# A gated cross-attention block: squared queries in bf16 halves, and the turns and the queue in a new order

## What is computed

```python
q = (layernorm(x) @ Wq).reshape(B, 100, 16, 128); k, v = ctx @ Wk, ctx @ Wv   # k, v likewise by head
q = q * rsqrt(mean(q * q, -1) + EPS) * gq
k = k * rsqrt(mean(k * k, -1) + EPS) * gk
x = x + tanh(g_xattn[0]) * (softmax(q @ k.T / sqrt(128)) @ v @ Wo)
x = x + tanh(g_ffn[0]) * bitlinear_ffn(layernorm(x))    # ternary weights, 8-bit activations
```

## Time and profile before

| | us |
|---|---|
| median of the runs | 2326.5 (2323.11 to 2329.4) |
| the profiled execution | 2321.96 |
| its span, first to last instruction | 2320.2 |
| PE busy in it | 2209.8 (95%) |
| DVE / ACT / POOL busy | 1820.5 / 1612.1 / 1265.4 |

### The profile page before, as it was taken

How to read it: one execution, slowest core, us unless ns; L and a number is a source line. 1 busy time by engine, 2 the same in 40 slices (tenths; PEclk the granted TensorE clock), 3 DMA queues, 4 the chain that set the end, 5 groups by cost and what they waited for, 6 DMA issues and landing times. The chain is left out here.

```text
span 2320.2 us, 45840 instructions
## 1 busy us (share of the span) xinstructions
PE 2209.8 (95%) x16338; PEld 1564.2 (67%) x16338; DVE 1820.5 (78%) x4171; ACT 1612.1 (69%) x3398; POOL 1265.4 (55%) x1623
## 2 busy tenths in 40 slices
PE   5799999999999999999999999999999999769999
PEld 3567777777777777777777777776777777524444
DVE  5888877777877777877787787777877777579996
ACT  4677777777776777777777677776777677446665
POOL 4555656565656565656667676766676655200000
PEclk9999999999999999999999999999999999989999
DMA  6777676766767677657776767677767665635655
GB/s 147 172 152 141 127 143 127 141 135 129 141 129 143 130 140 128 136 105 149 136 146 135 154 132 154 132 146 136 137 145 139 132 108 115 177 87 142 140 139 125
DMA packets 921748, 317.53 MB, mean 137 GB/s; under 512 B 864912, under 2 KB 882608, under 8 KB 921264
## 3 DMA queue, kind: packets, MB, share of 16 engines
q1 hardware_dynamic: 921520, 314.61, 67.5%
HBM read 82.09 MB, written 19.40 MB: 44 GB/s over the span
## 5 line engine op out<-in xcount | busy, mean ns | idle before, releaser
L893 DVE TENSOR_TENSOR khat<-keys_ps,krs 128x512 f32<-128x512 f32 (+1 forms) x384 | 263.6, 686 | 286.2 <-POOL krs L1175 286.2
L1181 POOL TENSOR_TENSOR ksplit<-khat,ksplit 128x512 bf16<-128x512 f32 (+1 forms) x384 | 444.6, 1159 | 70.7 <-ACT ksplit L667 68.7
L1175 POOL TENSOR_TENSOR krs<-kvar,minus_half 128x4 f32<-128x4 f32 (+1 forms) x384 | 387.1, 1008 | 32.0
L689 ACT ACTIVATE prob<-score_ps,nbias,qrs 100x361 f32<-100x361 f32 x512 | 329.1, 647 | 65.3 <-DVE nbias L911 63.6
L1172 POOL TENSOR_SCALAR kvar<-kss 128x4 f32<-128x4 f32 (+1 forms) x384 | 88.6, 231 | 513.6 <-DVE kss L883 511.4
L672 ACT ACTIVATE ksq<-keys_ps 128x512 f32<-128x512 f32 (+1 forms) x384 | 228.3, 596 | 196.2 <-PE keys_ps L25 196.2
L923 DVE SCALAR_TENSOR_TENSOR psplit<-prob,rden,psplit 100x361 bf16<-100x361 f32 x512 | 349.3, 690 | 5.5 <-ACT psplit L698 1.4
L698 ACT ACTIVATE psplit<-prob,rden 100x361 bf16<-100x361 f32 x512 | 304.1, 594 | 49.6 <-DVE rden L917 48.7
L23 PE MATMUL keys_ps<-wk_split,ctxT 128*128 128x512 bf16 (+1 forms) x768 | 294.5, 383 | 26.2 <-DMA ctxT<-nat 14.7
L901 DVE TENSOR_REDUCE nmax<-score_ps 100x1 f32<-100x361 f32 x512 | 268.2, 524 | 54.6 <-PE score_ps L25 54.1
L667 ACT ACTIVATE ksplit<-khat 128x512 bf16<-128x512 f32 (+1 forms) x384 | 240.5, 626 | 85.0 <-DVE khat L893 83.7
(11 more groups left out here) (132 smaller groups left out, 5256.7 us busy)
## 6 DMA issues: line engine op xcount, KB each, us to landing
stage<-in_ffn SPq DMA_DIRECT2D x96, 256.0 KB, 3.2
ctx_raw<-in_ctx SPq DMA_DIRECT2D x31, 256.0 KB, 3.4
xin<-in_x SPq DMA_DIRECT2D x32, 200.0 KB
res_rows<-in_x SPq DMA_DIRECT2D x32, 200.0 KB
x_rows<-res_rows SPq DMA_DIRECT2D x32, 200.0 KB
xin<-x_rows SPq DMA_DIRECT2D x25, 256.0 KB, 2.8
xres<-x_rows SPq DMA_DIRECT2D x25, 256.0 KB, 3.0
out<-xres SPq DMA_DIRECT2D x25, 256.0 KB, 2.0
```

The source lines that it names most:

```text
L689: act.activation(prob[:, h, :], score_ps[h % 2][0:SQ, 0:SK], ACT.Exp, bias=nbias[:, b, h:h + 1], scale=qrs[:, v // 2 % 2, r:r + 1], accum_ ...
L893: dve.tensor_tensor(khat[0:KV[t], k, :].rearrange("p (h d) -> p h d", h=G), keys_ps[k][0:KV[t], :].rearrange("p (h d) -> p h d", h=G), rs, ...
L1175: pool.tensor_tensor(krs[0:KV[t], k, :], kvar[0:KV[t], k, :], minus_half[0:KV[t], 0:G], ALU.pow).then_inc(krs_done, 1)
L1181: pool.tensor_tensor(ksplit[0:KV[t], t, 1, :], khat[0:KV[t], (u + t) % 2, :], ksplit[0:KV[t], t, 0, :], ALU.subtract).then_inc(k_lo_done, 1)
```

## The change

- **Squares in halves.** ACT squares each query half twice, once into fp32 (`qsq`, now for one half at a time) and once into bf16 (`queries_square_hi`). POOL subtracts the second from the first (`query_squares_lo`). `query_squares` then runs two bf16 matmuls a head and sample instead of one fp32 one, each with 128 columns of weights instead of 100, so that it reads 28 columns further than its data. The fp32 copy of y that is turned at a pair's end (`yT`) lies in the same memory.
- **Waits added.** `queries_lo` also waits for both squares. `queries_square` waits for POOL's low half of the half before. `scores` waits until the last `queries_lo` of its head group has freed its bank.
- **Order.** On PE, `queries(1)` stands before the third key tile and `keys(v + 2, 0)` right after it; the two mixes stand together; `query_squares` moves from in front of `heads_out` to in front of `project`; in the second turn two projections stand before the first scores. ACT, DVE and POOL follow. ACT's new order in two_turns: keys_square 0, 1; queries_hi 0, queries_square_hi 0; weight_chunk(u); queries_square 0; exp 0; keys_hi 0; queries_hi 1, queries_square_hi 1; keys_square 2; queries_square 1; keys_square(v) 0; probs_hi 0, exp 1; keys_hi 1; mixed_hi 0; keys_hi 2; mixed_hi 1; exp 2, probs_hi 1; keys_square(v) 1; exp 3; [turn_x_hi 0]; heads_out_hi 0, 1; [turn_x_hi 1]; probs_hi 2, 3; keys_square(v) 2, keys_hi(v) 0, 1; exp(v) 0, 1; keys_hi(v) 2; weight_chunk(v); probs_hi(v) 0, exp(v) 2, 3; mixed_hi(v) 0, 1; probs_hi(v) 1, 2, 3.
- **Queue.** Chunks have two buffers each way, a chunk is loaded a turn earlier and stored a turn later; context is loaded at the ends of turns 2 and 6 and turned in turns 4 and 5 behind the keys. The new buffers lie in the staging slots, of which there are now 6 instead of 7.

The core of the diff (indentation cut by 8):

```diff
 k = (AT_LAST if last else AT_LOOP)[key] + len(AT_FIRST)
 return i * USES + k, k % 2
+    def query_use(i, u):
+n = i * UNITS + u // 2 * 2 - 3
+return use(n // UNITS, ("q", n % UNITS, QD - 1))[0]
     def unit(i, u):
...
 qT_hi, qT_lo = sb("qT_hi", [P, 2, G, QT], BF16), sb("qT_lo", [P, 2, G, QT], BF16)
-qsq = sb("qsq", [P, G, QT], F32)
+qsq, qsq_split = sb("qsq", [P, TWO, QT], F32), sb("qsq_split", [P, 2 * G * QT + PAD], BF16)
+qsq_hi, qsq_lo = (qsq_split[:, a * G * QT:(a + 1) * G * QT].rearrange("p (h q) -> p h q", h=G)
+                  for a in range(2))
 psplit = sb("psplit", [SQR, QD, 2, TWO, SKF], BF16)
 oT_hi, oT_lo = sb("oT_hi", [P, G, QT], BF16), sb("oT_lo", [P, G, QT], BF16)
 assert NT == G
-yT = qsq
+yT = qsq_split[:, 0:2 * G * QT].bitcast(F32).rearrange("p (m q) -> p m q", m=NT)
 res_rows = sb("res_rows", [P, 2, DM], F32)
...
 assert CHUNK == PIECE
-w_raw, w_out = stage[:, 0, :], sb("w_out", [P, CHUNK], BF16)
-w_abs, w_part = sb("w_abs", [P, MATRICES, CHUNKS], F32), sb("w_part", [P, MATRICES], F32)
+w_raw, w_out = [stage[:, 0, :], stage[:, 3, :]], [
+    stage[:, 2, k * CHUNK // 2:(k + 1) * CHUNK // 2].bitcast(BF16) for k in range(2)]
...
+        i, u = (i, u + 1) if u < UNITS else (i + 1, 1)
         n, m = sum_chunk_of(i, u), tern_chunk_of(i, u)
-        if n is not None and n > 0:
-            sp.wait_ge(w_summed, n)
-        if m is not None:
-            sp.wait_ge(w_summed, MATRICES * CHUNKS)
-            if m > 0:
-                sp.wait_ge(w_rounded, m)
-        if n is not None or m is not None:
+        if (n if at_start else m) is not None:
+            c = n if m is None else MATRICES * CHUNKS + m
+            if m is not None:
+                sp.wait_ge(w_summed, min(c - 1, MATRICES * CHUNKS))
+                if m > 1:
+                    sp.wait_ge(w_rounded, m - 1)
+            elif n > 1:
+                sp.wait_ge(w_summed, n - 1)
             rows, cols = chunk_at(n if m is None else m)
-            sp.dma_start(w_raw[:, :], w_ffn[rows, cols]).then_inc(w_raw_in, 16)
+            sp.dma_start(w_raw[c % 2], w_ffn[rows, cols]).then_inc(w_raw_in[c % 2], 16)
...
+        m = tern_chunk_of(*((i, u - 1) if u > 1 else (i - 1, UNITS)))
         if m is not None:
             rows, cols = chunk_at(m)
             sp.wait_ge(w_rounded, m + 1)
-            sp.dma_start(w_tern[rows, cols], w_out[:, :]).then_inc(w_tern_out, 16)
+            sp.dma_start(w_tern[rows, cols], w_out[m % 2]).then_inc(w_tern_out[m % 2], 16)
     def load_ternary(u):
...
+        load_chunk(i, u, True)
         if not last and u == 1:
-            sp.wait_ge(nat_ready, (i * 2 + 2) * KVT)
-            load_ctx(i + 1, 0, ctx_raw)
             for b in range(2):
                 sp.wait_ge(xT_hi_done, i * 2 + b + 1)
                 load_x(i + 1, b, xin, x_in)
-        if not last and u == 3:
-            sp.wait_ge(nat_ready, (i * 2 + 3) * KVT)
-            load_ctx(i + 1, 1, ctx_raw)
-        if not last and u in (UNITS - 3, UNITS - 2):
-            sp.wait_ge(keys_done, tile(i, u + 1, KVT - 1) + 1)
-            turn_ctx(i + 1, u - (UNITS - 3), 1 - par)
         if has_keys(u, last):
             turn_keys(i, u + 2, 0), turn_keys(i, u + 2, 1), turn_keys(i, u + 2, 2)
+        if not last and u in (UNITS - 4, UNITS - 3):
+            sp.wait_ge(keys_done, tile(i, u + 2, KVT - 1) + 1)
+            turn_ctx(i + 1, u - (UNITS - 4), 1 - par)
         load_pieces(i, u, 0)
         if has_scores(u, last):
...
         if has_scores(u, last):
             turn_probs(i, u + 1, 1)
         load_pieces(i, u, 2)
+        if not last and u == 2:
+            sp.wait_ge(nat_ready, (i * 2 + 3) * KVT)
+            load_ctx(i + 1, 1, ctx_raw)
+        if i < PAIRS - 2 and u == UNITS - 2:
+            sp.wait_ge(nat_ready, (i * 2 + 4) * KVT)
+            load_ctx(i + 2, 0, ctx_raw)
         store_chunk(i, u)
+        load_chunk(i, u, False)
         if last:
             load_ternary(u)
...
             eng.wait_ge(kT_in[b], keys_turned(i, u))
+            eng.wait_ge(shared_free, query_use(i, u) + 1)
...
         ps = shared_bank(i, ("qss", u))
-        eng.wait_ge(q_sq_done, i * (NG * QD) + ((u + 3) // 2 + 1) * QD)
+        eng.wait_ge(q_sqlo_done, i * (NG * QD) + ((u + 3) // 2 + 1) * QD)
         for b in range(2):
             for h in range(G):
-                last = pe.matmul(ps[0:SQ, b * G + h:b * G + h + 1], qsq[:, h, b * SQ:(b + 1) * SQ],
-                                 ones[:, 0:1], start=True, stop=True)
+                out, hi, lo = ps[:, b * G + h:b * G + h + 1], h * QT + b * SQ, (G + h) * QT + b * SQ
+                pe.matmul(out, qsq_split[:, hi:hi + P], ones[:, 0:1], start=True, stop=False)
+                last = pe.matmul(out, qsq_split[:, lo:lo + P], ones[:, 0:1], start=False, stop=True)
         last.then_inc(shared_done, 1)
     def heads_out(i, u, k):
...
@@ -600,39 +627,36 @@
             queries(i, u, 0)
         if su:
             scores(i, u + 1, 0), scores(i, u + 1, 1)
+        if qu:
+            queries(i, u, 1)
         if ku:
             keys(i, u + 2, 2)
-        if qu:
-            queries(i, u, 1)
+        if kv:
+            keys(i, v + 2, 0)
         if su:
             scores(i, u + 1, 2)
-        mixed(i, u, 0, par)
+        mixed(i, u, 0, par), mixed(i, u, 1, par)
         if su:
             scores(i, u + 1, 3)
-        if kv:
-            keys(i, v + 2, 0)
-        mixed(i, u, 1, par)
         if kv:
             keys(i, v + 2, 1)
         if new_x:
             turn_x(i, 0)
-        if qu:
-            query_squares(i, u)
-        if i == TERN_PAIR - 1 and u == 1:
-            weight_totals(i)
         heads_out(i, v, 0), heads_out(i, v, 1)
         if new_x:
             turn_x(i, 1)
         if kv:
             keys(i, v + 2, 2)
+        if qu:
+            query_squares(i, u)
+        if i == TERN_PAIR - 1 and u == 1:
+            weight_totals(i)
+        project(i, v, 0), project(i, v, 1)
         if sv:
             scores(i, v + 1, 0), scores(i, v + 1, 1)
-        project(i, v, 0), project(i, v, 1)
-        if sv:
-            scores(i, v + 1, 2)
         project(i, v, 2), project(i, v, 3)
         if sv:
-            scores(i, v + 1, 3)
+            scores(i, v + 1, 2), scores(i, v + 1, 3)
         if mv:
             mixed(i, v, 0, par), mixed(i, v, 1, par)
         if v == UNITS:
...
         eng.wait_ge(shared_done, n + 1)
-        act.activation(qsq[:, k * TWO:(k + 1) * TWO, :],
-                       shared_ps[p][:, 0:TWO * QT].rearrange("p (h q) -> p h q", h=TWO),
-                       ACT.Square).then_inc(q_sq_done, 1)
+        if started(i * (NG * QD) + (u + 3) // 2 * QD + k):
+            eng.wait_ge(q_sqlo_done, i * (NG * QD) + (u + 3) // 2 * QD + k)
+        act.activation(qsq[:, :, :], ps, ACT.Square).then_inc(q_sq_done, 1)
+    def queries_square_hi(i, u, k):
+        n, p = use(i, ("q", u, k))
+        ps, heads = shared_ps[p][:, 0:TWO * QT].rearrange("p (h q) -> p h q", h=TWO), slice(k * TWO, (k + 1) * TWO)
+        eng.wait_ge(shared_done, n + 1)
+        act.activation(qsq_hi[:, heads, :], ps, ACT.Square).then_inc(q_sqhi_done, 1)
     def queries_hi(i, u, k):
...
         eng.wait_ge(q_hi_done, i * (NG * QD) + ((u + 3) // 2 * QD + k + 1))
+        eng.wait_ge(q_sq_done, i * (NG * QD) + ((u + 3) // 2 * QD + k + 1))
+        eng.wait_ge(q_sqhi_done, i * (NG * QD) + ((u + 3) // 2 * QD + k + 1))
...
@@ -1026,83 +1050,84 @@
         kv, sv, mv = has_keys(v, last), has_scores(v, last), has_mixed(v, last)
         new_x = u == UNITS - 5 and not last
         if ku:
-            sum_keys(i, u + 2, 0), scale_keys(i, u + 2, 0), sum_keys(i, u + 2, 1)
+            sum_keys(i, u + 2, 0), sum_keys(i, u + 2, 1)
         if su:
-            row_max(i, u + 1, 0), row_bias(i, u + 1, 0), row_max(i, u + 1, 1), row_bias(i, u + 1, 1)
+            row_max(i, u + 1, 0), row_bias(i, u + 1, 0), row_max(i, u + 1, 1)
+        if ku:
+            scale_keys(i, u + 2, 0)
         if qu:
             queries_lo(i, u, 0)
+        if ku:
+            scale_keys(i, u + 2, 1)
+        if su:
+            row_bias(i, u + 1, 1)
         if i == TERN_PAIR - 1 and u == 1:
             weight_sums()
-        if ku:
-            scale_keys(i, u + 2, 1), sum_keys(i, u + 2, 2)
         if su:
             row_sum(i, u + 1, 0)
         if ku:
-            scale_keys(i, u + 2, 2)
+            sum_keys(i, u + 2, 2)
+        if qu:
+            queries_lo(i, u, 1)
+        if kv:
+            sum_keys(i, v + 2, 0)
         weights_lo(pieces_of(i, u, 0))
         if su:
             row_max(i, u + 1, 2)
         if new_x:
             layernorm(i, 0)
-        if qu:
-            queries_lo(i, u, 1)
+        if ku:
+            scale_keys(i, u + 2, 2)
         if su:
-            row_max(i, u + 1, 3), row_bias(i, u + 1, 2), row_sum(i, u + 1, 1), probs_lo(i, u + 1, 0)
-            row_bias(i, u + 1, 3)
-        mixed_lo(i, u, 0)
-        if kv:
-            sum_keys(i, v + 2, 0)
```

(81 more changed lines are left out.)

139 lines of the change are left out of this document (69 added, 70 removed).

## The result

| | before | after |
|---|---|---|
| median of the runs, us | 2324.98 | 2438.47 (2435.8 to 2445.77) |
| ratio to before | | 1.049, interval 1.0461 to 1.0519 |
| span of the profiled execution | 2320.2 | 2444.0 |
| PE busy / idle in it | 2209.8 / 110.4 | 2182.0 / 262.0 |
| mean granted clock | 0.984 | 0.961 |

The change makes the kernel 4.9% slower, where 1.2% faster was forecast (2298 us, range 2262 to 2332). PE has less to do, as intended. But it stands idle for 151.6 us more by the trace. (The median of the four runs before is 2324.98, halfway between the middle two, and not the 2326.5 from which the forecast was counted. The 1.5 us change nothing in what follows.)

A forecast was written before the change was run, and what follows sets the result against it. PE's own work was taken to bound the kernel's body. Span 2320.2 - 28 (squares) - 4 (waits) + 4 (start and last unit) = 2292.2 us; from the median of 2326.5, 2298 us, range 2262 to 2332.

The forecast's parts named there:

- What bounds the kernel: Body from 150 to 1985 us runs at PE's own pace, with PE idle only 28.6 us there.
- The queue: SP's chunk stores and context loads move behind the transposes; second load buffer stops SP standing still; no cost taken.
- The added wait of `queries_lo`: DVE's queries_lo waits for both squares, all of DVE queued behind; ACT's wait for POOL covered by 0.6 us.
- `qvar`: PE's 10.3 us of waits for qvar go, as the sum's bank is needed some 8 us later.
- `khat` of the usual turns: PE's 4.1 us of waits for khat before key tiles go, with 0.9 us to spare.
- The x turn: PE waits for xT_lo before the second heads_out, about 1.4 us in each of 15, 21 us; bounds 0 and 2.1 each.
- The context's transposes: Three transposes ahead leave the second probability transpose about 0.6 us before need; no cost taken, bound 0.5 us x 15.
- The margin of 0.6 us on POOL: POOL's low half of the first square, behind a chunk's rounding, is ready 0.6 us before ACT's second square.
- The squares on PE: A bf16 pass takes 57 ns instead of 84, so a sum takes 0.91 us instead of 1.35; 28 us gained.
- Rival A: Faster weight load on PE: 30 ns a pass, 0.48 us a sum, 27 us more gained, 2271 us; chance 0.17.
- B: Rival: no gain on PE, 86 ns a pair holds at one moving column too, 2326 us; chance 0.14.
- Rival C: DVE backlog over the count makes PE wait before the next first key tile; at 0.8 us, +48, 2346 us; chance 0.17.

The follow-up runs named there:

- b_best: Changed kernel with chunk loads at the turn's start, first chunk of a pair of turns used later, turn_x halves earlier, second context transpose behind turn_probs: 2271.3 us.
- a_load: Changed kernel with only the ternary chunk's load issued at the start of the turn before its use, instead of at its end: 2340.41 us.
- a_use: Changed kernel, loads left late, with ACT's scaling of the first turn's chunk moved behind the fourth exponential and POOL's rounding moved later: 2320.74 us.
- a_mid: Changed kernel with the chunk load in the same turn, but behind the keys' and context's transposes and in front of both turn_probs: 2344.18 us.
- b_fp32: b_best with the fp32 sums of the kernel before: one square a half on ACT, no POOL subtraction, 16 passes with 100 weight columns: 2309.9 us.
- h_before: Kernel before with only the squares in bf16 halves, including their waits and staging slots; old order and old queue: 2337.59 us.
- b_ctx: a_load with only the second of the two context transposes moved behind turn_probs: 2297.67 us.

## Why the prediction was wrong, point by point

- **What bounds the kernel** was right as a reading of before, and b_best shows it still holds: PE's work and PE's waits make up the time. The forecast failed on the waits.
- **The queue: this is the step that failed.** "and the loads have a second buffer, so SP no longer stands still for a chunk", and at its end "No cost taken, 0.5 us x 15 as its bound". I weighed the chunk edit only as a relief for SP and, in a separate place, the rounding against POOL's chain. I never set the place of the load (behind the probabilities of the turn before, where it had in effect been) against the new place of its use on ACT (`weight_chunk(u)`, moved forward by some 9 us, more than the some 8 us by which the chunk had been early: 10.8 from issue to use, less its transfer). A second buffer allows an early load. It does not make one: the load goes out when SP's order gets to it. a_load, a_use and a_mid, each mending one side alone, give 98, 118 and 94 us, and after lies 113 us above before. Mending this step alone would not have made the forecast right, though: a_load is 42 us above it, with the squares worth 32 more than forecast. The rest are the terms below that were sized too small.
- **The added wait of `queries_lo`.** I named it ("behind which all of DVE is queued") but followed only POOL's low half into it. The chunk stands in front of the same `qsq`. It is this wait that carries ACT's stall on to DVE and PE.
- **`qvar`:** right. 11.6 us of waits fell to 1.5. **`khat` of the usual turns:** not gone as I had said. With the chunks mended 19 to 20 us in 30 to 35 short waits remain, where before had 11.3 us in the whole run; the 0.9 us to spare that I counted isn't there everywhere.
- **The x turn:** right in kind, too small. 29.8 us in 15, 2.0 a time where I took 1.4, close to the upper bound of 2.1. With the chunk's stalls gone (a_load) it is 36.1 us, 2.4 a time and over the bound.
- **The context's transposes:** the bound of 0.5 us x 15 was too low. `pT` was late once a pair of samples, in a_load by 1.5 to 3.4 us, 2.4 on average, and 43.3 us with the one long wait (7.0) that before has too (5.3). I counted three transposes in front of the second probability transpose, and gave the place 0.6 us of cover, less than such a count can tell.
- **The margin of 0.6 us on POOL:** not there. ACT waited 26.7 us for the low half in a_load (18 times, 1.5 us each). POOL's low half takes 943 ns, as estimated (0.9), so it is the sequence that was laid too tight. POOL's 1374.6 us are near the 1381 that I had given. ACT's 1640.0 are not: they are 28 us more than before and not 64, though its 128 added squares last 501 ns each. Between b_best and b_fp32, which differ in the squares alone, ACT's busy time differs by 47.6 us.
- **The squares on PE:** the largest term on the side of gain, mis-sized by a factor of two: 60 us instead of 28, since a pass takes 25.5 ns and not 57. My argument from the load records split 98 ns into 41 of latency and 57 that repeats. In truth nearly three quarters of the 98 ns are latency (98 - 25.5 = 72.5). Rival A's pass of 30 ns was the nearest, B (86 ns a pair) is refuted. The number of records was wrong as well: the passes are 64 x 16 = 1024, as I had counted them at first, and not 2048. The gain does not arrive whole: PE's busy time fell by 27.8 us by the trace and by some 17 with the missing records put in. The 43 us that are missing fit the lower granted clock, as worked out below.
- **Rival C:** its place was right (K0' waiting for `khat`) and so was the side. Its cause was not. I had it as DVE's backlog in all 60 pairs of turns; the waits lie in the 24 pairs of turns with ternary chunks and go with the chunk's load. At 97.1 us in 22 between 1085 and 1900 us, 4.4 each (some 4.0 without the missing record) where C had 0.8, they are also beyond the price that I allowed. C's chance of 0.17, with a range that left it out, was too low a figure for an order in which five margins of 0.6 to 0.9 us had each been counted.
- **Two slips in the working.** The forecast's own lower bound should have been 2298 - 21 - 3 = 2274 and not 2286, by its bounds for the x turn and the start. And a pair of turns takes 122 / 4 = 30.5 us by the places of `turn_y`, not 29.2. Neither changes the outcome.

How the loss divides can be estimated. A granted clock of 0.961 over 2444.0 us and of 0.984 over 2320.2 are 95 and 37 us of full speed lost, so the lower clock could take 58 us more from PE; since PE is idle in part of that time, the 43 us by which its busy time is longer than the squares would leave it fit this. That makes +141 (idle) - 60 (squares) + 43 (clock) = +124, the difference of the spans. No run has the waits without the clock, so the 43 are worked out and not shown by themselves. What stays open is the share of the added waits in h_before, and which part of a_use's further 20 us is POOL's.

## What to carry to other kernels

Where a change moves the use of a loaded buffer forward, or its load back, find the load in the queue that issues it and read what the instructions ahead of it wait for; a second buffer helps only as far as that order lets the load go early. Compare two distances, from issue to use before the change and after it. Price a new wait by what is queued behind the waiting instruction on its engine, and not by the wait: 35.7 us of ACT's waits cost next to nothing in one order, 154.4 cost over 100 us in the other. And when an operation becomes shorter, list what it had been covering: a sum of squares 0.94 us faster made the kernel slower where it stood and 38.6 us faster once the order was made for it.

## What the runs showed of the hardware

**A pass of one moving column costs some 25.5 ns with new weights each time.** Weight loads of after by form (instruction, count, busy us in total, mean ns of one, idle time ahead):

```profile
L554 PEld LDWEIGHTS shared_ps<-ones,qsq_split 128*128 128x128 bf16 x512 | 31.6, 96 | 14.3 <-DVE oT_lo L899 4.9 <-issue 3.2 <-DVE qT_lo L980 1.4
```

A load's record lasts 96 ns and yet 16 loads and matmuls start within 0.41 us. The record is therefore mostly latency that overlaps with the next, and says little of the rate. The same 16 passes with fp32 and 100 columns take 84 ns each. The Trainium skill (TensorE: Matmul & The Clock Gate, Back-to-back issue gap) puts pairs of load and matmul at some 81 ns where N, the moving side, is 128, and gives a floor of some 25 ns for a single matmul of 1 to 64 moving columns. The trace agrees with that floor, here for pairs: 25.5 ns with one moving column. The prediction had read the 128 as columns of weights, so its 81 ns spoke of another shape and not against the change.

**A stall of PE has a second price.** After some 4.2 us without work its granted clock was 0.50 (1.2 GHz), and matmuls of 512 columns stood 0.43 us apart instead of 0.21. Between 1060 and 1985 us, 56 windows of 2 us were under 0.8 in after, 12 in a_load, 7 in b_best and none in b_ctx. Against a_load b_ctx has 24.4 us less idle time, and PE is busy for 19.0 us less with the same work. The clock lost 54 us of full speed in a_load ((1 - 0.977) x 2335.1) and 32 in b_ctx ((1 - 0.986) x 2291.7), a difference of 22, enough for the 19.
